# A recurrent cell in a nine-stage kernel: input rows added by TensorE, one of eight products done ahead for all four cells

## What is computed

```
def _lstm_activate(gates, c):
    i, f, g, o = jnp.split(gates, 4, axis=-1)
    c_new = sigmoid(f) * c + sigmoid(i) * tanh(g)
    h_new = sigmoid(o) * tanh(c_new)
...
def step(carry, x_t):
    h, c = carry
    logits = concatenate([h, c, x_t]) @ W_sel.T + b_sel
    onehot = one_hot(argmax(logits), 4)
    g_all = einsum('bi,sgi->bsg', x_t, W_ih) + einsum('bh,sgh->bsg', h, W_hh) + b_ih + b_hh
    g = einsum('bsg,bs->bg', g_all, onehot)
    h2, c2 = _lstm_activate(g, c)
```

## Time and profile before

| | |
|---|---|
| median of the runs | 6420.35 us |
| the profiled execution, its own time | 6423.3 us |
| its span | 6421.3 us |
| mean granted TensorE clock | 0.945 |
| TensorE products busy | 5387.0 us, 84% |
| VectorE busy | 3158.5 us, 49% |
| ScalarE busy | 1088.2 us, 17% |
| GpSimd busy | 613.4 us, 10% |
| `lstm_steps`, about 2300 to 5685 us | about 3380 us, 53% of the span |
| `lstm_inputs`, about 1898 to 2198 us | about 300 us |

### The profile page before, as it was taken

One profiled execution on the slowest core, in us unless ns is written; L12 is line 12 of the kernel. 1 busy time (PEld: TensorE's weight loads), 2 busy tenths in 40 slices (PEclk: granted clock), 3 DMA queues, 4 the chain that ended last, 5 costly groups with the idle time before them and its releaser, 6 DMA issues. The chain is left out here.

```text
span 6421.3 us, 214665 instructions
## 1 busy us (share of the span) xinstructions
PE 5387.0 (84%) x84946; PEld 3259.0 (51%) x84948; DVE 3158.5 (49%) x13265; ACT 1088.2 (17%) x4645; POOL 613.4 (10%) x1014
## 2 busy tenths in 40 slices
PE   8997878849989658888888888888888888878778
PEld 6543443324657435555555555555555555544444
DVE  4402443214541365555555555555555555555543
ACT  0000000012321131111111111111111111122312
POOL 0000750003630000000000000000000000001100
PEclk9998989979999879999999999999999999989877
DMA  0000111566433400000000000000000000000010
GB/s 10 26 26 10 40 41 39 120 173 209 120 97 130 182 16 5 10 5 5 5 5 10 5 5 5 5 5 10 5 5 5 5 10 0 0 23 36 14 62 8
DMA packets 128787, 240.28 MB, mean 37 GB/s; under 512 B 47084, under 2 KB 64114, under 8 KB 127687
## 3 DMA queue, kind: packets, MB, share of 16 engines
q1 hardware_dynamic: 68584, 146.72, 6.5%
q0 software_dynamic: 60128, 92.58, 5.7%
HBM read 165.58 MB, written 73.29 MB: 37 GB/s over the span
## 5 line engine op out<-in xcount | busy, mean ns | idle before, releaser
L1457 PE MATMUL bank<-lstm_w,step_h_parts 128*32 128x128 f16 (+1 forms) x59904 | 1229.7, 237 | 327.8 <-issue 327.8
L1457 PEld LDWEIGHTS bank<-lstm_w,step_h_parts 128*32 128x32 f16 x59904 | 1109.1, 97 | 648.4 <-issue 634.5
L1427 PE MATMUL bank<-lstm_w 128*128 128x512 f16 x4992 | 1296.7, 382 | 3.3 <-issue 3.3
L1481 DVE TRANSPOSE_TENSOR_REDUCE step_summed<-bank 128x4 f32<-128x128 f32 x1872 | 670.6, 358 | 299.5 <-PE bank L1457 278.9
L1427 PEld LDWEIGHTS bank<-lstm_w 128*128 128x128 f16 x4992 | 386.3, 98 | 388.8 <-issue 5.1
L1406 ACT ACTIVATE step_act_out<-step_gates 128x4 f32<-128x4 f32 x625 | 128.6, 206 | 2124.2 <-DVE step_gates L1487 2120.8
L1534 DVE COPY step_xgs<-step_xg 128x16 f32 x624 | 109.0, 175 | 731.1 <-issue 705.3
L1487 DVE SCALAR_TENSOR_TENSOR step_gates<-step_summed,lstm_inv_scale,step_xgs 128x4 f32<-128x4 f32 x1872 | 414.9, 222 | 64.8
L1396 POOL COPY xnT<-step_state 128x4 f32 (+1 forms) x625 | 116.5, 186 | 3317.3 <-DVE step_state L1514 3317.3
L1109 PE MATMUL bank<-sum_parts,sum_hot 125*125 125x512 f16 x1600 | 347.6, 381 | 6.7 <-DVE sum_parts L1068 6.7
L1437 PE MATMUL bank<-lstm_wsel,step_state 128*1 128x4 f32 x4992 | 214.9, 168 | 110.7 <-DVE step_state L1504 110.7
(11 more groups left out here) (368 smaller groups left out, 6617.4 us busy)
## 6 DMA issues: line engine op xcount, KB each, us to landing
rel_h<-rel_h_sb SPq DMA_DIRECT2D x39, 1024.0 KB, 4.3
lstm_xg<-xg_g POOLq DMA_DIRECT2D x4, 5000.0 KB, 19.5
step_xg<-lstm_xg SPq DMA_DIRECT2D x25, 800.0 KB, 4.4
xg_w<-in_c_w_ih SPq DMA_DIRECT2D x8, 2048.0 KB, 10.8
lstm_w<-in_c_w_hh SPq DMA_DIRECT2D x4, 4096.0 KB, 31.0
rel_z<-rel_z_sb POOLq DMA_DIRECT2D x8, 1250.0 KB, 22.9
rel_zg<-rel_z POOLq DMA_DIRECT2D x8, 1248.0 KB
cheb_w<-in_L_gnn_weight SPq DMA_DIRECT2D x8, 1024.0 KB
```

What stands on the lines that cost most here:

```text
L1427: nc.tensor.matmul(idle[:], w[:, 0, 0, 0, 0, 0:128], w[:, 0, 0, 0, 0, :], start=True, stop=True)
L1457: last = nc.tensor.matmul(bank[32 * q:32 * q + 32, 0:32 * (end - first)], h_parts[:, c, :], w[:, s, c, q, a, 32 * first:32 * end], start=( ...
L1481: nc.vector.tensor_reduce(summed[:, first:end], bank[:, 0:32 * (end - first)].rearrange("p (b r) -> p b r", r=32), X_AXIS, ALU.add, apply_ ...
```

## The change

**Inputs.** The layout of `B.xg` becomes 16 groups (gate f, g, i, o by 32-row strip) of rows of 512 values (four cells by 128), each value as three bf16 parts that add up to the f32 value. `lstm_inputs` makes 80 products (16 groups by five tiles of 125 rows), rows stationary and weights streaming 512 columns; VectorE does three passes per product, ScalarE two, and GpSimd issues 80 stores of 375 KB. The two biases are loaded broadcast to 125 partitions, 4 MB each, behind the first weight tile.

**Steps.** The gates lie in four banks, one for each gate, and each bank has the columns of all four cells. At the start of a step four products of 512 columns (`inject`) write the input rows of all four cells, scaled up, into the banks. After the low half of h is there, the first of the eight products is added for all four cells (64 products of 128 columns: `halves[:HALVES_AHEAD]`), and after the pick the other seven for the chosen cell. The unused products are gone. VectorE reduces 128 columns of each bank at the chosen cell; `add_input` and the copy of the input row are gone, and ScalarE applies the scale inside its activation, on `summed`. The position in the ring (`t % 15`) and the wait for its refill (`t // 5`) are computed by TensorE's sequencer. At the start of the block VectorE clears the ring (128x7680 bf16) before the first refill.

```
-WARM_PICK, WARM_GATES = 4, 4
+HALVES_AHEAD = 1
...
+            def inject(part, at, stop):
+                p, bank, _, _ = part
+                return nc.tensor.matmul(bank[:], rows[:, p, :], xg[:, at], start=True, stop=stop)
+
+            def add_half(part, s, c, a, stop):
+                p, bank, _, _ = part
+                for q in range(4):
+                    last = nc.tensor.matmul(bank[32 * q:32 * q + 32, 128 * s:128 * s + 128], h_parts[:, c, :],
+                                            w[:, s, c, q, a, 128 * p:128 * p + 128], start=False, stop=stop,
+                                            tile_position=(0, 32 * q))
+                return last
...
             with pe.Fori(1, STEPS) as t:
 
+                pe.wait_ge(xg_loaded, (t // XG_CHUNK + 1) * 16)
+                at = bass.ds((t % XG_RING) * 512, 512)
+                for part in parts:
+                    pe.wait_ge(part[3], t)
+                    last = inject(part, at, stop=False)
+                last.then_inc(injected, 1)
                 pe.wait_ge(init, 1)
                 pe.wait_ge(input_score_ready, t)
...
                 last.then_inc(score_done, 1)
-                keep_clock_up(WARM_PICK - 1)
                 pe.wait_ge(init, 1)
                 pe.wait_ge(h_lo_ready, t)
-                keep_clock_up(1)
+                for s in range(CELLS):
+                    for part in parts:
+                        for c, a in halves[:HALVES_AHEAD]:
+                            add_half(part, s, c, a, stop=False)
...
                 def cell(s):
...
+                    for part in parts:
+                        for c, a in halves[HALVES_AHEAD:]:
+                            last = add_half(part, s, c, a, stop=(c == KC - 1 and a == 1))
+                        last.then_inc(part[2], 1)
...
-                keep_clock_up(WARM_GATES)
...
-            def add_rows(part, t):
-                first, end, bank, done, summed_part, _ = part
-                dve.wait_ge(done, t)
-                nc.vector.tensor_reduce(summed[:, first:end], bank[:, 0:32 * (end - first)].rearrange(
+            def add_rows(part, s, n):
+                p, bank, done, summed_part = part
+                dve.wait_ge(done, n)
+                nc.vector.tensor_reduce(summed[:, 4 * p:4 * p + 4], bank[:, bass.ds(s * 128, 128)].rearrange(
                     "p (b r) -> p b r", r=32), X_AXIS, ALU.add, apply_transpose=True).then_inc(summed_part, 1)
-
-            def add_input(part, t):
...
-                nc.vector.tensor_copy(xgs[:], xg[:, bass.ds(s, 1), bass.ds((t % RING) * GC, GC)]
-                                      ).then_inc(xgs_ready, 1)
```

274 lines of the change are left out of this document (142 added, 132 removed).

## The result

The changed kernel takes 6505.43 us (median of 4 runs, 6502.11 to 6509.85); the kernel before, beside it on the same chip, 6421.31 us (6419.92 to 6422.92). The ratio is 1.0131, with a 95% interval of 1.0114 to 1.0149: 84 us slower, where 104 us faster was forecast. The profiled execution of the changed kernel took 6502.1 us with a span of 6500.4 us.

A forecast was written before the change was run, and what follows sets the result against it. TensorE's chain through the exposed loop end and injections was to bound each step, not c. From 6423.3 us, 112 less for the steps and 8 more for input stage and start gave 6319, as run median 6316 us; range 6200 to 6440.

The forecast's parts named there:

- the sum of TensorE's chain from the jump to L: Step's end on TensorE: jump at 1.32, injections from 2.22, last product for the choice (L) at 3.53 us, before 3.71.
- the 5 us for the input stage: Input stage: 5 us more than before, between -5 and +20, mainly from bias loading ahead of the second weight tile.
- the 1.68 us from L to the next cell: Step's tail: last product for the choice to next cell stays 1.68 us, products ahead hidden by 0.02 us.
- rival 5: TensorE's clock falls to 1.2 GHz, some 2.5 us more a step; chance 0.04 together with rival 4.
- rival 4: TensorE's loop code no longer fits and is fetched every step: +2290 us, 8700 us; chance 0.04 together with rival 5.
- 0.90 us from the jump: TensorE's loop end: time from the jump out of the cell to the first injection, register work included.
- upper bound of 1.1 us: TensorE's loop end: jump to first injection if division and remainder cost what VectorE pays, 0.231 us each.
- c at 2.37: VectorE and ScalarE: new c 2.37 us from the cell's start, 0.63 earlier than before, without setting the step's end.
- The biases and the sum take some 23 + 9 us: Input stage's start: loading and adding 8 MB of biases; TensorE's six banks cover about 20 us, 5 to 12 stay open.
- Rival 6: Steps already wait elsewhere, so the change gains only 0.00 to 0.03 us a step, within 0.2%; chance 0.06.
- Rival 3: Register addresses slow the four injections, 0.28 us each; step 0.13 longer, 6509 us; chance 0.14.
- Rival 2: Products ahead hold up the pick, giving back 0.15 us a step; about 6409 us; chance 0.10.

The follow-up runs named there:

- s2_two_more: Changed kernel with two more unread products of 512 columns behind the four injections of each step: 6780.5 us.
- s5_static: Changed kernel with injections streaming from a fixed address, no ring refill or register computations (part of the computation left out): 6399.5 us.
- s12_plain_scale: Activation scale made a program constant, on a kernel with injections at the step's end, VectorE's loop turned, and o's products behind the pick: 6281.8 us.
- i4_deeper: Changed kernel with biases loaded and added in 16 pieces and eight input-stage buffers instead of four for values and parts: 6426.2 us.
- s1_early: Changed kernel with the next step's four injections and their register work moved ahead of the jump out of the cell: 6402.5 us, ratio 0.9975.
- s3_ahead0: Changed kernel with none of a cell's eight products done ahead of the pick (HALVES_AHEAD 0): 7306.8 us.
- s7_before_nogates: Kernel before without the unused products that fill TensorE's wait for c (WARM_GATES 0 instead of 4): 6746.5 us.

## Why the prediction was wrong, point by point

Forecast and result are 189 us apart (6316 and 6505). About 108 of them are the gain of the steps that didn't come and about 76 the input stage; the rest is within the scatter of the runs. Two steps of the prediction failed: the sum of TensorE's chain from the jump to L, which came out 0.21 us too short, and the 5 us for the input stage, which had the load of the biases at a third of its time and no term for the stores.

**Right.** The sequencer's lead of 0.2 us and the jump at 1.32 (measured 1.33); the cell's last product at 1.52 (1.54); the fourth injection 0.66 behind the first (0.66); TensorE and not c at the end of a step (s2_two_more); the 1.68 us from L to the next cell (1.66), with the products ahead hidden in the changed kernel; the branch back, 209 ns where 207 was read before. The Trainium skill (Advanced Engine Details and Errata, Control Flow Timing) gives about 108 ns for such a branch; the measured duration decides. The clock stayed at 1.00 (rival 5). And the loop's code is not fetched again (rival 4): the table of DMA queues of the changed kernel from 2410 to 5750 (packets, MB, share) has one row, the refills of the ring, and none for instructions:

```profile
q1 hardware_dynamic: 7808, 29.99, 3.4%
```

The two cache lines of which the Trainium skill speaks (Runtime: NRT & Kernel Launch, Instruction fetch mechanics) set no limit here.

**Wrong in size: the tail of TensorE's chain.** The mechanism of the sum was right, and three of its terms were each too small. The step was to gain 0.18 us; L came 0.21 us later than predicted (3.74 against 3.53).
- "0.90 us from the jump" was 0.99 in the steps that have this jump (2.31 - 1.32; three of the four ways out of the cell). s5_static splits it: 0.68 for jump, addition, branch and move, where I had 0.60, and 0.31 for the register work, where I had 0.30. So the guessed term held and the one read from rows didn't: I had taken 0.05 off the 0.65 of the rows for the hand-over to the array, where 0.03 come on top. (The prediction's upper bound of 1.1 us adds up to 1.03 from its own terms; the forecast doesn't use it.)
- The fourth injection to L took 0.80 and not 0.65. I had put the small products 0.025 apart straight behind the injection's last column. The timeline shows two gaps that the sum lacks. The injections start at 3503.34, the fourth 0.66 later, and its columns pass until 3504.21, but the first small product starts at 3504.31. Two products at 0.025 would let the next group start at 3504.36; it starts at 3504.42. That makes 0.10 and 0.06, together the missing 0.15. The sequencer's waits don't make these gaps. It has passed the one ahead of the first small product (L1483) by 3503.42 and the last one that the trace shows ahead of the second and third groups (L1489) by 3503.93. What makes them no run shows.

```profile
L1483 PEldq EVENT_SEMAPHORE  x1: 51/51/51, 3503.4 to 3503.4; - x1
```
```profile
L1489 PEldq EVENT_SEMAPHORE  x1: 51/51/51, 3503.9 to 3503.9; - x1
```

- The cell's last product was 0.02 later than the sum had it.

These make 0.26 where there is the jump, and 0.21 in the mean, since 129 steps leave the cell without one and have L at 3.55. The kernel before has its L at 3.75 in the mean, where the one step that I read had 3.71. So of 0.18 us of gain 0.21 are lost and 0.04 come back; in the mean 0.005 is left. A forecast of 112 us stood on a difference of 0.18 between two chains of 3.5 us, and no term of it had a margin for small gaps. The range had one (a gain of 0.05 to 0.35), and the result was a little outside it.

**Wrong in size, without effect: c at 2.37.** It came at 2.57. The activations with a scale from memory take 298 ns and not 206, which moves c by 0.11 (s12_plain_scale); the rest is that of the reductions, which start 0.11 late: the first starts 0.73 us into the cell, where I had 0.62. The prediction put their register addresses into the time before 0.62 and between the reductions; in the trace each is computed after the wait for the products (L1526 above).

**Wrong: the input stage, +5 predicted, +81 measured.** "The biases and the sum take some 23 + 9 us" took a landing time of a 4 MB load of another kind. The two biases are one row each, read for 125 partitions. The traffic of the changed kernel from 1880 to 2290, in 40 slices:

```profile
GB/s 1 151 158 145 165 137 131 141 80 19 175 151 191 121 198 145 167 209 109 218 117 187 112 181 169 160 213 102 208 113 198 145 166 82 122 105 109 117 162 451
```

While the biases come in (slices 2 to 8, up to 1962) the rate is 131 to 165 GB/s; in the last slice, where the recurrent weights load, it is 451. At some 150 GB/s the 8 MB and two weight tiles take 65 to 70 us. Why it is slow, the table by stretch tells for three stretches of the changed kernel: the biases alone, the recurrent weights, and the load of the array at the kernel's start (columns as in the earlier trace rows; the last two are the busy share of the 16 DMA engines and GB/s):

```profile
1952.00:1962.00 10.00, 0.00 (x0) 0.00 (x0) 0.00 (x0) 0.00 (x0) 0.00 (x0) 0.50 0.32 138
2277.00:2289.00 12.00, 0.00 (x0) 0.00 (x0) 0.82 (x1) 0.00 (x0) 0.00 (x0) 0.50 1.00 415
7.00:12.00 5.00, 0.00 (x0) 0.00 (x0) 0.00 (x0) 0.00 (x0) 0.00 (x0) 1.00 0.33 129
```

The biases keep 0.32 of the 16 engines busy, which is 5 of them, and the weights all 16. The packets aren't slower: most of 32 KB take 1.21 us in both. Nor is it the one row read 125 times: the load of the array reads each row once, and it too runs on 5 engines at 129 GB/s. What it shares with the biases is that it goes to 125 partitions, while the weights go to 128; no run changes that number.

For the stores the sum had no term at all: it counted what the engines do with a tile, 2.1 us of VectorE against 3.5 of TensorE, but not how long the tile keeps its buffer, 8.5 us of landing above all. i4_deeper, which has neither fault, has products of 277.6 us, where 278 was predicted, and its time is 5 us above the kernel before, where the sum has 8 and a gain in the steps that didn't come.

**Of the rivals** none was it. Rival 6 (no change in the steps) describes them, but by balance and not by a wait elsewhere. Rival 3's number, 6509 us, is within 4 us of the result, and its mechanism didn't happen: the injections stand 0.22 us apart. Rival 2, the products ahead, didn't bind in the changed kernel and did as soon as anything else was mended: s1_early was expected at 6225 and took 6402 for it and for VectorE's branch.

## What to carry to other kernels

Work that is put into a wait is free only until the wait's end, and with each limit that is taken away the next stands close behind: write down for each chain of a step when it is ready, not only the one that is last, and expect a gain only down to the second. A tile's buffer is held from its first write until its store has landed; divide that time by the number of buffers and compare it with the tile's own time on the bounding engine, with the slowest landing and not the median. (An estimate for the changed kernel: five passes of 0.6 to 0.7 us, 1.3 of issue and 8.5 of landing are 13 us, or 3.3 a tile with four buffers against TensorE's 3.5, which looks enough; with its slowest landing, 12.2, it is 4.2.) Before unused products are taken away, say what fills their gap instead, since the clock depends on it.

## What the runs showed of the hardware

- Without work in one wait of each step TensorE's granted clock fell to 0.77 (s3_ahead0) and 0.86 (s7_before_nogates), and stood at 1.00 with the wait filled, whether by useful or by unused products; the clock alone cost 649 and 327 us.
- An activation on 128x4 values takes 298 ns with a scale from memory and 205 ns with a constant.
- Loads to 125 partitions kept 5 of the 16 DMA engines busy (138 GB/s for the biases, 129 for the array at the start), a load to 128 partitions all 16 (415 GB/s in the stretch shown, 451 in the fastest slice).
- VectorE's reduction at a register's address started 0.11 us later than at a fixed one would by the rows of the kernel before: the address is computed after the wait (57 ns for the first, 40 ns for the others).
- From the last column of a product of 512 columns to the first small product in f32 it took 0.10 us, and between the first two groups of small products 0.06 us more than their spacing, with no wait of the sequencer in the trace in either.
- TensorE's sequencer was 0.2 us ahead of the array in the cell's products and 0.6 us ahead in the four injections, so its lead is not one fixed time.
- A loop of about 1090 instructions of TensorE, by the prediction's count, ran 624 times with no instruction fetch in the trace.
